# Decoder kernel, fused cross attention and router loop: key rotation over three steps, router work in step 7, narrower scores

## Chip, cores and metric

The kernel runs on one core of one Trainium2 chip, as a single program. The metric is the device time of one execution in microseconds, the median of several runs.

## What is computed

Two decoder blocks over eight sequences (B = 8) of 256 tokens of width 256, with 64 context tokens each. In order: a linear state mixer, cross attention to the context and a ternary-weight gated FFN (block 0); causal self attention, an attention over context and tokens, and a mixture of 32 experts (block 1). The change lies in the last attention and the router of the experts:

```python
q = rms_norm((x @ wq).reshape(B, L, 16, 128), q_norm_w)
k = rms_norm((x @ wk).reshape(B, L, 4, 128), k_norm_w)
k_ctx = rms_norm((h_ctx_kv @ wk_ctx).reshape(B, T, 4, 128), k_norm_w)
q = q * cos + rotate_half(q) * sin
k = k * cos + rotate_half(k) * sin
k_full = concatenate([k_ctx, k]); v_full = concatenate([v_ctx, v])   # 64 + 256 keys
scores = einsum("blhd,bmhd->bhlm", q, k_full) / sqrt(128) + causal mask on the last 256
out = softmax(scores) @ v_full @ wo
x = x + out
...
logits = einsum("bsd,ed->bse", layernorm(x), router_w)     # 32 experts
top1_w, top1_idx = max(softmax(logits)), argmax(logits)
```

## The kernel before

Six phases follow each other: mixer, cross attention, FFN, self attention, **hybrid** (cross attention with rotary keys, and beside it the router of earlier batches), experts. Each engine has its own program, written out by hand; semaphores hold them together. What stands in what order is set by the `hybrid` function of each engine (VectorE L879, POOL L1229, ScalarE L1563, TensorE L2068). Batches 0 to 2 are unrolled, batches 3 to 6 run in a hardware loop of two batches per turn, batch 7 follows it in the same body's last form.

**Units and steps.** A batch has eight steps `i`. Unit `u = 8 * b + i` is one half of the tokens (`j`, steps 0 to 3 and 4 to 7) and one group of four heads (`g`). In step `i` TensorE issues, in this order: scores of tiles 0 and 1 of unit u + 1; the raw query of unit u + 3 (`raw_query`, 4 matmuls of 512 columns); outputs of unit u - 2; scores of tiles 2 and 3 of u + 1; the turned query of u + 2; the turned probabilities of u - 1. In steps 4 and 7 stands `hybrid_out` as well (32 matmuls of 256 columns): in step 4 for the second half of the batch before, in step 7 for the first half of this one. VectorE in step `i`: copies of turned probabilities of u - 2 (L765 to L767), `masked_max` of tiles 0 and 1 of u + 1 (L746), `finish_query` of u + 2 (L728, L732), `normalise` of u (L755, L758), the step's extra work, `masked_max` of tiles 2 and 3, `rotate_query` of u + 3 (L716, L722). Scores lie in two PSUM banks, so the next step's scores wait for the masked maximum of this one; the raw query has one bank, so it waits for the rotation of the one before.

**Tiles of scores.** A tile is 32 tokens by four heads against its keys. `WIDTHS` (L20) gives how many keys each of the four tiles gets: 128, 128, 192, 192 in the first half and 256, 256, 320, 320 in the second. `kmask` adds -1e30 to keys that the token must not see.

**Keys of the next batch.** Three tiles: k = 0 the context (64 keys), k = 1 and k = 2 the tokens. POOL squares and scales them, VectorE sums the squares (`square_key`, L633) in steps 2 to 4 and rotates (`turn_key`, L636), TensorE turns (`turn_keys`, L1865), ScalarE copies the turned tile to its place (`turned_keys`, L1453). Before, VectorE has k = 0 and 1 in step 4 and k = 2 in step 5; TensorE and ScalarE have k = 0 and 1 in step 5 and k = 2 in step 6.

**Router.** For batch b - 1 VectorE has `hybrid_finish` (the residual addition, L772) and `token_stats` (L780, L784) in step 4 and `keep_scales` (L793) in step 6; POOL `token_scales` in step 5; ScalarE `token_norm` (L1544) in step 5. For batch b - 2: TensorE turns the tokens in step 2 and multiplies by the router weights (`route`, 8 matmuls of 32 columns) in step 4; VectorE has `copy_logits` (L799) late in step 5, `choose` (L805 to L816, maximum and index) in step 6 and `keep_weight` (L823) in step 7; ScalarE the exponentials (`weights`) in step 7. In step 5 TensorE waits for the copy of the logits (`f_lg`) ahead of the turned probabilities, since both use bank 7.

## Time and profile before

| what | value |
|---|---|
| median of 3 runs | 1252.36 us (1252.36 to 1252.71) |
| the profiled execution | 1250.75 us, span 1248.9 us |
| TensorE matmul busy | 1060.5 us, 85% of the span |
| VectorE busy | 894.2 us, 72% |
| ScalarE busy | 645.0 us, 52% |
| POOL busy | 324.4 us, 26% |
| one batch of the hybrid loop (885.9 to 970.3) | 84.4 us |

The hybrid phase runs from about 482 to 1156 us. The profile gives each instruction with its start, its length, the idle time of its engine before it and what ended that idle time. In the rows PE is TensorE, DVE is VectorE, ACT is ScalarE; L1663 is the helper that issues every matmul, told apart by its operands (`PS<-wq` raw query, `PS<-wo` hybrid_out, `PS<-EW,arena` scores, `PS<-rwT` router). A matmul's recorded length contains its way through the array, so a rate is read from the distance of starts.

### The profile page before, as it was taken

Reading aid. Unit: us, or ns where it says so; the run is one execution under the profiler, and the core shown is the slowest. Engines: PE = TensorE matmul, PEld = TensorE weight load, DVE = VectorE, ACT = ScalarE, POOL = GpSimd, SP = SyncE. Lnnn points to the kernel's source line nnn. Section 1 sums busy time; section 2 is a strip of 40 time slices with the busy share of each in tenths; the row PEclk is TensorE's granted clock in tenths of the full one; section 3 lists DMA queues with packets and bytes.
Section 4 is the critical chain, followed back from the end, with each engine's and each line's share of the span. In section 5 each row is a group of like instructions: output and inputs, shape, how many; then the busy total and the mean of one; then the engine's idle time right before and its main releaser. Section 6 shows DMA issues by size and latency. Waiting matters only on the chain.

```text
span 1248.9 us, 22083 instructions
## 1 busy us (share of the span) xinstructions
PE 1060.5 (85%) x6399; PEld 729.9 (58%) x6407; DVE 894.2 (72%) x2522; ACT 645.0 (52%) x2011; POOL 324.4 (26%) x496
## 2 busy tenths in 40 slices
PE   3676788689989967989999999899999998998396
PEld 1444345566666644556666666666656666665285
DVE  4576677487788765886867967778678678665375
ACT  0434777455555633655556545555565555552262
POOL 0212321211232121322313213223133132111456
PEclk9955999999999988989999999999999999999598
DMA  9501000112122000400000000000000000000731
GB/s 306 202 0 34 1 1 1 51 53 52 51 58 84 27 1 4 146 1 13 1 6 9 1 14 1 1 14 1 6 9 1 13 1 1 13 1 16 256 91 47
DMA packets 38795, 49.58 MB, mean 40 GB/s; under 512 B 5030, under 2 KB 29484, under 8 KB 38448
## 3 DMA queue, kind: packets, MB, share of 16 engines
q1 hardware_dynamic: 36400, 44.31, 11.9%
q0 software_dynamic: 2304, 4.24, 1.0%
q8 instruction: 35, 0.57, 0.2%
q14 instruction: 56, 0.46, 0.1%
HBM read 32.70 MB, written 14.78 MB: 38 GB/s over the span
## 4 chain that ended last, share of the span: by engine, by line
PE 37%; DVE 11%; issue 6%; POOL 3%; ACT 3%; DMA 0%; DVEq 0%; ACTq 0%; POOLq 0%
PE PS L1663 33%; POOL out_dram L1289 3%; DVE arena L746 2%; DVE arena L758 1%; DVE arena L722 1%; PE PS L2011 1%; PE PS L1988 1%; ACT arena L1505 1%; POOL tokens_dram L1265 1%; ACT arena L1514 1%; DVE arena L732 1%; DVE arena L728 1%; DVE small L780 0%; DVE early L655 0%; DVE early L650 0%
## 5 line engine op out<-in xcount | busy, mean ns | idle before, releaser
L1663 PE MATMUL PS<-EW,arena 128*128 128x128 f32 (+4 forms) x640 | 134.4, 341 | 18.0 <-DVE small L746 11.2
L1663 PE MATMUL PS<-early,arena 128*32 128x256 f32 (+6 forms) x856 | 105.1, 357 | 42.1 <-DVE early L612 23.7
L1663 PE MATMUL PS<-wq,EW 128*128 128x512 f32 x256 | 126.6, 617 | 12.6 <-DVE arena L722 12.3
L1203 POOL TENSOR_SCALAR small<-small 128x4 f32<-128x4 f32 x64 | 18.3, 286 | 427.4 <-ACT mask L1498 250.4
L1663 PEld LDWEIGHTS PS<-EW,arena 128*128 128x128 f32 x640 | 99.6, 193 | 48.9 <-issue 23.5
L746 DVE CUSTOM_DVE_ANT_0 arena<-PS,kmask 128x128 f32<-128x128 f32 (+3 forms) x256 | 92.4, 389 | 42.3 <-PE PS L1663 34.1
L1514 ACT ACTIVATE arena<-arena,small 128x128 f32<-128x128 f32 (+3 forms) x256 | 119.5, 471 | 1.3 <-DVE small L751 1.1
L1505 ACT ACTIVATE arena<-PS 128x512 f32<-128x512 f32 x64 | 38.2, 597 | 153.2 <-PE PS L1988 153.2
L1663 PE MATMUL PS<-wo,early 128*128 128x256 f32 x512 | 113.3, 380 | 2.5 <-DVE sinT L799 1.7
L1663 PEld LDWEIGHTS PS<-wo,early 128*128 128x128 f32 x512 | 97.2, 190 | 16.3 <-DVE sinT L799 2.1
L1663 PEld LDWEIGHTS PS<-early,arena 128*32 128x32 f32 (+3 forms) x864 | 49.8, 115 | 93.3 <-issue 45.5
L1498 ACT ACTIVATE mask<-PS 128x128 f32<-128x128 f32 x256 | 66.7, 274 | 48.5 <-PE PS L1663 47.8
L680 DVE TENSOR_REDUCE small<-PS 128x4 f32<-128x512 f32 x64 | 58.2, 951 | 43.2 <-PE PS L1663 43.2
L1107 POOL TENSOR_SCALAR ve<-mv 128x2 f32<-128x2 f32 x40 | 8.9, 222 | 281.4 <-DVE mv L378 281.0
L1663 PEld LDWEIGHTS PS<-wq,EW 128*128 128x128 f32 x256 | 45.4, 192 | 57.7 <-issue 41.9
L1205 POOL TENSOR_TENSOR small<-small,halves 128x4 f32<-128x4 f32 x64 | 70.3, 1098 | 5.3
L758 DVE TENSOR_SCALAR arena<-arena,small 128x128 f32<-128x128 f32 (+3 forms) x256 | 68.8, 333 | 2.3
L1663 PE MATMUL PS<-arena,EW 128*128 128x512 f32 (+1 forms) x160 | 63.7, 510 | 3.3 <-ACT arena L1521 2.1
L1440 ACT ACTIVATE early<-PS 128x384 f32<-128x384 f32 x64 | 28.5, 488 | 71.3 <-PE PS L1892 71.3
L1479 ACT ACTIVATE arena<-PS,small 128x256 f32<-128x256 f32 x128 | 63.0, 493 | 0.0
L1478 ACT ACTIVATE arena<-PS,small 128x128 f32<-128x128 f32 x128 | 48.8, 381 | 25.7 <-DVE small L680 25.0
L2011 PE MATMUL PS<-ident,arena 128*128 128x128 f32 x384 | 52.8, 274 | 8.3 <-DVE sinT L799 8.3
(310 smaller groups left out, 2467.3 us busy)
## 6 DMA issues: line engine op xcount, KB each, us to landing
EW<-in_masksT_dram SPq DMA_DIRECT2D x32, 256.0 KB, 3.4
tokens_dram<-EW SPq DMA_DIRECT2D x1, 4160.0 KB, 14.9
arena<-tokens_dram SPq DMA_DIRECT2D x16, 260.0 KB, 3.0
results_dram<-EW SPq DMA_DIRECT2D x32, 128.0 KB, 3.2
EW<-results_dram SPq DMA_DIRECT2D x4, 1024.0 KB, 10.5
X<-in_x_dram SPq DMA_DIRECT2D x1, 2048.0 KB, 8.8
wq<-in_wq_dram SPq DMA_DIRECT2D x1, 2048.0 KB, 11.8
wo<-in_wo_dram SPq DMA_DIRECT2D x1, 2048.0 KB, 18.8
```

The lines of the kernel that those rows point to most:

```text
L680: last = dve.tensor_reduce(d_neg[:, i % 2, j, :], PS[:, 0:4, at:at + n], AX.X, ALU.max, negate=True)
L746: dve.tensor_tensor_reduce(probs(i, t), PS[:, 3 + t % 2, 0:n], kmask[:, at:at + n], 1.0, LOWEST, ALU.add, ALU.max, e_max[:, t:t + 1]).then ...
L758: last = dve.tensor_scalar(probs(i, t), probs(i, t), e_inv[:, t:t + 1], None, ALU.mult)
L1205: pool.tensor_tensor(e_rqs[:, i % 2, :], e_q3[:, i % 2, :], halves[:, 0:GH], ALU.pow).then_inc(e_rq, 1)
L1289: pool.indirect_dma_start(out_rows[:, :], bass.IndirectOffsetOnAxis(ap=to, axis=0), sY[:, k, t, :], None, bounds_check=B * S - 1, oob_is_e ...
L1478: act.activation(dP[:, i % 2, r, 0:P], PS[:, r, 0:P], ACT.Exp, bias=d_neg[:, i % 2, 0, r:r + 1])
L1479: act.activation(dP[:, i % 2, r, P:3 * P], PS[:, r, P:3 * P], ACT.Exp, bias=d_neg[:, i % 2, 1, r:r + 1]).then_inc(d_e, 1)
L1498: last = act.activation(eSQ[:, h * XD:(h + 1) * XD], PS[:, 1, h * XD:(h + 1) * XD], ACT.Square, accum_out=e_q2[:, i % 2, h:h + 1])
L1505: act.activation(eQT.rearrange("p (t h q) -> p h t q", t=4, h=GH), PS[:, 2, :].rearrange("p (h t q) -> p h t q", t=4, h=GH), ACT.Copy).the ...
L1514: last = act.activation(tile, tile, ACT.Exp, bias=e_neg[:, i % 2, t:t + 1], accum_out=e_sum[:, i % 2, t:t + 1])
L1663: return pe.matmul(dst, lhs, rhs, start=first, stop=last)
L2011: pe.transpose(PS[:, 5 + k, t * P:(t + 1) * P], eP[:, i % 4, at:at + P], ident[:, :])
```

## The change

- `SEEN` gives the scores' products 96, 128, 160 (first half) and 224, 256, 288 (second half) columns for tiles 0 to 2; tile 3 and everything that reads the scores keep `WIDTHS`.
- `turn_key` (VectorE): k = 0 in step 4, k = 1 in step 5, k = 2 in step 6.
- `turn_keys` (TensorE) and `turned_keys` (ScalarE): k = 0 in step 5, k = 1 in step 6, k = 2 in step 1 of the batch that uses it, in bank 7. TensorE waits for that copy in step 2.
- `token_stats`, `choose` and, behind `hybrid_finish`, `keep_weight` in step 7, `keep_scales` for batch b - 2 in step 1, `copy_logits` at the start of step 5. In the last batch `token_stats` stays in step 4 and `keep_scales` in step 6.
- `token_scales` (POOL) in step 7, `token_norm` (ScalarE) for batch b - 2 at the end of step 0, `weights` ahead of the copied outputs in step 7. In the last batch the first two stay in step 5.

```diff
+SEEN = ((96, 128, 160, 192), (224, 256, 288, 320))
...
+                    if i == 5 and routed:
+                        copy_logits(b - 2, 7)
...
                     if i == 4:
                         if nxt[0] == HYBRID:
                             turn_key(nxt[1], 0)
-                            turn_key(nxt[1], 1)
                         if former:
                             hybrid_finish(b - 1, 1)
+                            if nxt[0] != HYBRID:
+                                token_stats(b - 1)
+                    if 5 <= i <= 6 and nxt[0] == HYBRID:
+                        turn_key(nxt[1], i - 4)
+                    if i == 1 and routed:
+                        keep_scales(b - 2)
+                    if i == 6 and nxt[0] != HYBRID:
+                        keep_scales(b - 1)
+                    if i == 7:
+                        if former and nxt[0] == HYBRID:
                             token_stats(b - 1)
-                    if i == 5 and nxt[0] == HYBRID:
-                        turn_key(nxt[1], 2)
-                    if i == 5 and routed:
-                        copy_logits(b - 2, 7)
-                    if i == 6 and former:
-                        keep_scales(b - 1)
-                    if i == 6 and routed:
-                        choose(b - 2)
-                    if i == 7:
                         if routed:
+                            choose(b - 2)
+                        if nxt[0] == HYBRID:
+                            hybrid_finish(b, 0)
+                            if routed:
+                                keep_weight(b - 2)
+                        else:
                             keep_weight(b - 2)
-                        hybrid_finish(b, 0) if nxt[0] == HYBRID else hybrid_last(b)
+                            hybrid_last(b)
...
-                    if i == 5 and former:
+                    if i == (7 if more else 5) and former:
                         token_scales(b - 1)
...
-                        turned_keys(nxt[1], 1 - par, 2)
+                        turned_keys(nxt[1], 1 - par, 1)
...
-                    if i == 5 and more:
-                        turned_keys(nxt[1], 1 - par, 1)
+                    if i == 1 and former:
+                        turned_keys(b, par, 2, 7)
                     if further[2]:
                         turned_query(u + 2)
-                    if i == 5 and former:
+                    if i == 0 and routed:
+                        token_norm(b - 2)
+                    if i == 5 and not more:
                         token_norm(b - 1)
...
-                        product(PS[:, 3 + t % 2, 0:WIDTHS[j][t]], eQT[:, t * P:(t + 1) * P],
-                                eKT[:, par, g, 0:WIDTHS[j][t]]).then_inc(e_s, 1)
+                        product(PS[:, 3 + t % 2, 0:SEEN[j][t]], eQT[:, t * P:(t + 1) * P],
+                                eKT[:, par, g, 0:SEEN[j][t]]).then_inc(e_s, 1)
...
+                    if i == 1 and former:
+                        turn_keys(b, 2, 7)
...
-                    if i == 5 and more:
-                        pe.wait_ge(e_kc, 3 * b + 4)
-                        turn_keys(nxt[1], 1)
```

How the order of instructions moves, at three places of the loop. Line numbers of the changed kernel are one higher on VectorE and eleven higher on TensorE.

VectorE, end of step 4, before (the rotation of the token tile ends, then the residual addition into X, the statistics, the masked maximum):

```order
L655 TENSOR_TENSOR early<-early 128x512
L658 TENSOR_TENSOR early<-early,small 128x512
L771 ISA
L772 ISA
L772 TENSOR_TENSOR X<-X,PS 128x256
L253 REGISTER_ALU
L207 REGISTER_ALU
L780 ISA
L780 BN_STATS small<-X 128x6 x2
L784 BN_AGGR small<-small 128x2 x2
L207 REGISTER_ALU
L746 ISA arena,small<-PS,kmask 128x320
```

and in the changed kernel (L659 is the last of the context tile's rotation, L773 the addition, L747 the masked maximum):

```order
L659 TENSOR_TENSOR early<-early,small 64x512
L772 ISA
L773 ISA
L773 TENSOR_TENSOR X<-X,PS 128x256
L208 REGISTER_ALU
L747 ISA arena,small<-PS,kmask 128x320
```

The token tile's rotation and the statistics no longer stand around the addition.

VectorE, step 6, before (normalise ends, then keep_scales and choose; the masked maximum follows behind the last row):

```order
L758 TENSOR_SCALAR arena<-arena,small 128x320 x2
L792 REGISTER_ALU
L793 ISA
L793 COPY X<-small 128x2x2
L805 MAX small<-sinT 128x8 x2
L808 TENSOR_SCALAR small<-small 128x2
L810 MAX_INDEX small<-small,sinT 128x8 x2
L813 CAST small<-small 128x2
L816 ISA
L816 TENSOR_SCALAR b_v<-iota,small 128x32
L816 ISA
L816 TENSOR_SCALAR b_v<-iota,small 128x32
```

and in the changed kernel (L647 to L659 are a rotation):

```order
L759 TENSOR_SCALAR arena<-arena,small 128x320 x2
L647 TENSOR_TENSOR early<-early,cosk 128x512
L651 TENSOR_TENSOR early<-early,sink 128x4x64 x2
L655 REGISTER_ALU
L656 TENSOR_TENSOR early<-early 128x512
L659 TENSOR_TENSOR early<-early,small 128x512
L208 REGISTER_ALU
L747 ISA arena,small<-PS,kmask 128x320
```

A rotation stands where keep_scales and choose stood.

TensorE, step 1, before (outputs, the context's keys and values of the next batch, the scores of tile 2):

```order
L1663 MATMUL PS<-arena,w_in 128x512 x2
L1663 MATMUL PS<-arena,w_in 128x256
L1850 REGISTER_ALU
L1663 MATMUL PS<-wvc,eCT 64x512
L1663 MATMUL PS<-wkc,eCT 64x512
L1663 MATMUL PS<-wvc,eCT 64x512
L1663 MATMUL PS<-wkc,eCT 64x512
L253 REGISTER_ALU
L1663 MATMUL PS<-EW,arena 128x192
```

and in the changed kernel (L1876 is `turn_keys`):

```order
L1674 MATMUL PS<-arena,w_in 128x512 x2
L1674 MATMUL PS<-arena,w_in 128x256
L208 ISA
L1876 MATMUL PS<-ident,early 128x128 x4
L1861 REGISTER_ALU
L1674 MATMUL PS<-wvc,eCT 64x512
L1674 MATMUL PS<-wkc,eCT 64x512
L1674 MATMUL PS<-wvc,eCT 64x512
L1674 MATMUL PS<-wkc,eCT 64x512
L254 REGISTER_ALU
L1674 MATMUL PS<-EW,arena 128x160
```

The four transposes of the third tile are new here, and tile 2 has 160 columns in place of 192.

## Rows read from the trace of the kernel before

**Rows 1.** Busy time by stretch, one batch: us, busy us (x) of each engine, PEclk, DMA, GB/s.
```profile
885.90:970.30 84.40, 79.35 (x356) 53.78 (x356) 64.60 (x213) 45.85 (x173) 22.49 (x33) 1.00 0.02 6
```

**Rows 2.** Timeline of TensorE, steps 4 to 7 (start, us, line, op, count [idle before]).
```profile
940.67 7.07 PE L1663 MATMUL PS<-wo,early 128*128 128x256 f32 x32
...
947.58 1.36 PE L1663 MATMUL PS<-EW,arena 128*128 128x320 f32 x6
...
950.41 1.13 PE L1663 MATMUL PS<-EW,arena 128*128 128x256 f32 x4 [0.49 <-DVE small L746]
...
952.38 1.98 PE L1663 MATMUL PS<-wq,EW 128*128 128x512 f32 x4 [0.45 <-DVE arena L722]
...
959.21 1.09 PE L2011 MATMUL PS<-ident,arena 128*128 128x128 f32 x8 [1.49 <-DVE sinT L799]
...
970.34 1.12 PE L1663 MATMUL PS<-wq,EW 128*128 128x512 f32 x2 [1.07 <-DVE arena L722]
```

**Rows 3.** The same timeline, step 0's raw query and step 4's router products.
```profile
901.27 1.88 PE L1663 MATMUL PS<-wq,EW 128*128 128x512 f32 x4
902.99 2.31 PE L1663 MATMUL PS<-arena,w_in 128*128 128x512 f32 x6
...
936.77 0.97 PE L1663 MATMUL PS<-rwT,XT 128*128 128x32 f32 x8
937.58 1.96 PE L1663 MATMUL PS<-wq,EW 128*128 128x512 f32 x4
```

**Rows 4.** Timelines of ScalarE and TensorE, step 1.
```profile
993.89 0.60 ACT L1521 ACTIVATE arena<-PS 128x512 f32<-128x512 f32 x1 [0.30 <-PE PS L2013]
...
996.31 1.88 PE L1663 MATMUL PS<-arena,EW 128*128 128x512 f32 x4
```

**Rows 5.** Timeline of VectorE, batch 1, steps 5 and 6.
```profile
622.09 0.69 DVE L646 TENSOR_TENSOR early<-early,cosk 128x512 f32<-128x512 f32 x1
...
624.83 0.48 DVE L746 CUSTOM_DVE_ANT_0 arena<-PS,kmask 128x320 f32<-128x320 f32 x1
...
631.69 0.20 DVE L793 COPY X<-small 128x4 f32<-128x4 f32 x1
632.23 0.49 DVE L746 CUSTOM_DVE_ANT_0 arena<-PS,kmask 128x320 f32<-128x320 f32 x1 [0.34 <-PE PS L1663]
```

**Rows 6.** Timeline of VectorE in the loop, steps 4 and 6.
```profile
947.91 0.42 DVE L772 TENSOR_TENSOR X<-X,PS 128x256 f32 x1 [2.07 <-PE PS L1663]
...
949.85 0.49 DVE L746 CUSTOM_DVE_ANT_0 arena<-PS,kmask 128x320 f32<-128x320 f32 x1
...
950.27 0.48 DVE L746 CUSTOM_DVE_ANT_0 arena<-PS,kmask 128x320 f32<-128x320 f32 x1
...
966.01 0.20 DVE L793 COPY X<-small 128x4 f32 x1
...
967.81 0.49 DVE L746 CUSTOM_DVE_ANT_0 arena<-PS,kmask 128x320 f32<-128x320 f32 x1
```

**Rows 7.** Batch 0: timelines of TensorE and VectorE, and the stretch at half clock.
```profile
534.50 2.05 PE L1663 MATMUL PS<-EW,arena 128*128 128x256 f32 x4 [3.59 <-DVE small L746]
...
539.68 0.18 DVE L755 RECIPROCAL small<-small 128x4 f32<-128x4 f32 x1 [0.81 <-ACT arena L1514]
...
551.32 0.49 DVE L746 CUSTOM_DVE_ANT_0 arena<-PS,kmask 128x320 f32<-128x320 f32 x1 [0.55 <-PE PS L1663]
...
534.50:541.00 6.50, 6.50 (x13) 3.49 (x14) 5.54 (x19) 2.54 (x10) 0.00 (x0) 0.50 0.01 3
```

**Rows 8.** Timeline of VectorE, batch 2, step 6.
```profile
713.60 0.17 DVE L793 COPY X<-small 128x4 f32<-128x4 f32 x1
...
715.02 0.48 DVE L746 CUSTOM_DVE_ANT_0 arena<-PS,kmask 128x320 f32<-128x320 f32 x1
```

**Rows 9.** Timeline of TensorE, last batch, steps 5 and 7.
```profile
1117.97 1.09 PE L2011 MATMUL PS<-ident,arena 128*128 128x128 f32 x8 [0.81 <-DVE sinT L799]
...
1131.67 1.56 PE L1663 MATMUL PS<-wo,early 128*128 128x256 f32 x6 [1.75 <-DVE sinT L799]
```

More of the change, by code:

```diff
@@ L1590, in hybrid @@
                         query_squares(u + 3, (i + 3) % 8)
+                    if i == 7 and routed:
+                        weights(b - 2)
                     if i >= 2:
@@ L1596, in hybrid @@
                         values(b, par, 1)
-                    if i == 7 and routed:
-                        weights(b - 2)
                     if i == 1 and more:
@@ L2092, in hybrid @@
                     if i == 6 and more:
-                        turn_keys(nxt[1], 2)
+                        turn_keys(nxt[1], 1)
                     if further[3]:
@@ L2108, in hybrid @@
                         keys(nxt[1], 1 - par, 1)
+                    if i == 2 and former:
+                        pe.wait_ge(e_kc, 3 * b + 3)
                     if i == 2 and routed:
@@ L2137, in hybrid @@
                         if i == 5 and more:
+                            pe.wait_ge(e_kc, 3 * b + 4)
+                        if i == 6 and more:
                             pe.wait_ge(e_kc, 3 * b + 5)
-                        if i == 6 and more:
-                            pe.wait_ge(e_kc, 3 * b + 6)
                         if i == 7:
```

## The prediction

> **What bounds the kernel now.** The change touches one phase, the hybrid loop (eight batches of eight steps), so I read the stretches first. A batch in the loop takes 84.4 us, and in it TensorE is busy for 79.35, VectorE for 64.60 and ScalarE for 45.85, at the full granted clock [rows 1]. TensorE paces the loop, with about 5 us per batch in which it stands. The timeline of TensorE shows where [rows 2]: 0.49 before the scores at the start of step 5, 0.45 before that step's raw query, 1.49 before its turned probabilities and 1.07 before the raw query of step 7. Each time the idle time is ended by VectorE: by its masked maximum (L746), its query rotation (L722) and the copy of the logits (L799). So a batch has two parts. From the raw query of step 7 (970.34) to the end of hybrid_out in step 4 (940.67 + 7.07 = 947.74) TensorE sets the time. From there to the next such raw query, 22.6 us, VectorE runs without a pause worth naming and sets it. The two parts have to be costed apart. The end of the second one is what decides the batch.
>
> **TensorE's part: one thing more, one thing less.** The four transposes of the third key tile move from the second part (where TensorE waits anyway) to step 1 (where it doesn't). A matmul instruction of 512 columns takes (902.99 - 901.27) / 4 = 0.43, or 0.84 ns a column [rows 3]. Four transposes of 128 columns therefore add 4 x 0.107 = 0.43 to this part.
>
> The shorter scores take 32 columns from tiles 0 and 2 of every unit; a product is two instructions, so each shortened tile saves 2 x 32 x 0.84 ns = 0.054. That holds for 192, 256 and 320 columns. For tile 0 of the first half (128 to 96) I count nothing: the router's eight products of only 32 columns still take (937.58 - 936.77) / 8 = 0.101 each, almost what 128 columns cost [rows 3], so a floor other than the columns holds there. The Trainium skill, TensorE: Matmul & The Clock Gate, section "Back-to-back issue gap", gives the isolated gap as growing with the columns alone down to 64, by which 96 columns would save that 0.054 too, some 1.7 us in all over 32 units; the same section says that this under-counts where each matmul has a weight load of its own, and the router's row bears that out. In this part fall one shortened tile each of the units scored in steps 7, 0 and 2, two of step 3 and one of step 4; that of step 1 saves nothing, because TensorE then waits for ScalarE's copy of the raw keys. Six times 0.054 is 0.32. TensorE's part becomes 0.43 - 0.32 = 0.11 **longer** per batch.
>
> What else lies in this part is covered. ScalarE's layer norm of the tokens (two instructions, 1.1 us) moves into step 0 ahead of the copy at 993.89, which moves by some 0.8 to 1.1; TensorE's products that read it start at 996.31, so it still lands over 0.7 ahead [rows 4]. If that cover were gone, the excess would be added to every batch. The copy of the turned third tile (0.6) sits in step 1 between the raw keys and the turned query, where ScalarE waits for TensorE. VectorE's keep_scales, and token_stats, choose and keep_weight in step 7, lie beside hybrid_out, for which VectorE waits there anyway; only keep_weight, a reciprocal of two columns, comes behind it, where the next scores are held by TensorE's own turned probabilities.
>
> **VectorE's part in the loop.** Start to start, turn_key of a full tile takes 624.83 - 622.09 = 2.74 [rows 5]. In step 4 it now does one small turn_key beside hybrid_out, then hybrid_finish and at once the masked maximum. Before, that began at 949.85, its second half at 950.27 [rows 6]. Now the second half waits for its scores, which end at 947.58 + 1.36 = 948.94; the hand-over from TensorE to VectorE took 0.17 at hybrid_finish (947.74 to 947.91), so it starts at 949.11. VectorE gains 1.16 us (with token_stats gone, 1.52 was the most it could gain). Through step 5 it keeps them: one full turn_key and one copy of the logits as before, the copy only earlier. TensorE's stands of 0.49 and 0.45 vanish. That of 1.49 loses its releaser, but the next scores need the masked maximum that stands behind turn_key, so it moves there rather than going away. In step 6 keep_scales and choose took 967.81 - 966.01 = 1.80; a turn_key of 2.74 stands in their place, 0.94 more. So the raw query of step 7 comes 1.16 - 0.94 = 0.22 earlier against hybrid_out, and the batch changes by 0.11 - 0.22 = -0.11. Four periods (between the raw queries of step 7 of batches 2 to 6): **-0.4**.
>
> **The other batches.** Batch 0 did both turn_keys in step 4 without a hybrid_out to cover them: TensorE stood 3.59 us, its granted clock fell to 0.50 (1.2 GHz) for the 6.5 us behind, and VectorE then waited 0.81 for ScalarE [rows 7]. With one turn_key per step the same work is spread, that wait and the later one of 0.55 for scores go, and with them what the second half of a masked maximum there waited (0.15) and 0.1 of overlap: **-1.6**, between 0.8 (the first alone) and 1.8. Batch 1 had no choose in step 6, only a short copy and 0.34 of waiting (631.69 to 632.23) [rows 5]: 2.74 - 0.54 = 2.20 more, less 0.15 that the maximum itself no longer waits, less the gain of step 4, here taken as 1.0 (unrolled code has fewer register instructions, so there is less to save; 0.8 to 1.16 in the range): +1.05, with TensorE's 0.11 **+1.2**. Batch 2 had choose, unrolled, in 715.02 - 713.60 = 1.42 [rows 8]: 2.74 - 1.42 - 1.0 + 0.11 = **+0.4**. Batch 7 turns no keys; its 0.81 stand for the logits goes [rows 9], but choose then stands ahead of the copy that releases hybrid_out at 1131.67: 0.3 less, and 0.1 for the third tile: **-0.2**.
>
> The sum is -0.4 - 1.6 + 1.2 + 0.4 - 0.2 = -0.6 us. The profiled execution took 1250.75 us, so it becomes 1250.1; the runs' median of 1252.36 lies 1.6 above the profiled one, so I forecast **1251.7**.
>
> **Rivals.**
> *VectorE hands over later (slower).* The place is the raw query of step 7. The lead won in step 4 has to exceed 0.94 + 0.11 = 1.05; I have 1.16. If something else holds the masked maximum of step 4 or ScalarE's exponentials of step 5 or 6 hold normalise, the lead is eaten and turn_key in step 6 is paid in full. With no lead at all the loop's four periods cost +1.05 each, batch 1 +2.2, batch 2 +1.4, less 1.8 for batches 0 and 7: +6.0, or **1258.4**. For it: the margin is 0.11, and VectorE's chain is unbroken. Against it: no row shows another waiter in step 4. Chance 0.17 (half of the loss would give 1255).
> *TensorE paces all (faster).* If VectorE's longer step 6 were absorbed, the stands of 0.49, 0.45 and 1.49 would all be gained, 2.4 less 0.1 in each of six periods, with batches 0 and 7 some -15 us: **1237**. For it: VectorE is busy only 64.60 of 84.40. Against it: it can't run ahead, since each masked maximum needs the scores of its own step, and its free time lies beside hybrid_out. A part of it is more likely than the whole; chance 0.15.
> *The clock falls.* In the second part TensorE now stands mostly before steps 6 and 7, 1.6 to 1.9 us at a time. A stand of 3.59 was followed by the half clock [rows 7], ones of 1.49 and 1.75 were not [rows 2, 9]. Were 6.5 us at half clock to follow in seven batches, ahead of or in the hybrid_out of step 7, that is 7 x 3.2 = 23 us: **1274**. The Trainium skill, TensorE: Matmul & The Clock Gate, section "HAM oscillation — how this bites in real kernels", tells that an engine that idles between bursts starts each burst at the slow clock; the trace agrees only for the long stand. Chance 0.03.
> *The scores don't get shorter in time*, because the weight loads hold the others too, as they do at 128 columns: +0.32 a batch, +2.3 in all: **1254.0**. Chance 0.07.
>
> **Chances and range.** The forecast's own case has 0.58; its unknowns (the lead in batches 1 and 2, step 6 in the loop, the end) make it 1249 to 1254.5. A measurement of this kernel can tell about 0.2%, 2.5 us. Faster by more: 0.15 and 0.07 of the forecast's case, 0.22. Slower by more: 0.17, 0.03 and 0.07, 0.27. No change: 0.51. The range, with the near halves of the two main rivals, is 1247.5 to 1257.
>
> **What would show it.** In the loop: no stand before the scores of step 5; one of 1.5 to 2 us before the scores of step 6, ended by L747; the raw query of step 7 still waiting about 1 us for the rotation; hybrid_out of steps 7 some 84.3 apart; in batch 0 no half clock near 534; batch 1 longer than 80.9 by about 1. Tile 0's scores of 96 columns as far apart as those of 128. If the spacing of batches moves by more than 0.4 either way, the balance of step 4's gain against step 6's loss was mis-sized; if a wait on ScalarE stands before the turned probabilities or products of step 1, the cover of its moved work was misjudged.

## The result, and the profile after

The changed kernel takes 1261.49 us (median of 4 runs, 1260.17 to 1263.67) beside 1252.53 of the kernel before: ratio 1.007, 95% interval 1.0052 to 1.0087. It is **slower by 9 us**, 4.5 beyond the range's upper end. The profiled execution took 1261.01 (span 1259.1).

I cut both traces at TensorE's raw query in step 7. "Hybrid phase" below is the time from the phase's first raw query to the end of its last hybrid_out: 683.70 before, 691.93 after, so +8.23. (In the 14 traces of this study the phase begins between 470.2 and 476.0 and what follows it takes 91.5 to 93.0, without relation to the kernel; so I compare the phase, and leave what remains of a profile's difference to that spread. Neighbouring batches of the loop differ by up to 0.3 us in the kernel before and by more in the changed one, so a batch is compared with the same batch.)

| stretch | forecast | measured | of it at half clock |
|---|---|---|---|
| batch 0 to its step 7 | -1.6 | -1.90 | none |
| to step 7 of batch 1 | +1.2 | +1.82 | none |
| to step 7 of batch 2 | +0.4 | +0.82 | none |
| four periods of the loop | -0.4 | +4.95 | 1.66 + 1.58 |
| from step 7 of batch 6 on | -0.2 | +2.55 | 1.42 + 1.65 |
| sum | -0.6 | +8.24 | 6.3 |

The largest part is the clock. Busy time by stretch of the changed kernel (us, then busy us and count of PE, PEld, DVE, ACT, POOL, the granted clock, DMA, GB/s), first two loop batches, then the 4 us behind five raw queries of step 7, then the last batch's hybrid_out of step 7:

```profile
892.08:978.32 86.24, 80.53 (x357) 54.36 (x357) 64.67 (x213) 45.43 (x173) 22.29 (x33) 0.98 0.02 6
978.32:1063.07 84.75, 79.03 (x356) 53.72 (x356) 64.43 (x213) 45.53 (x173) 22.53 (x33) 1.00 0.02 5
...
721.30:725.00 3.70, 3.70 (x5) 1.45 (x5) 3.59 (x14) 0.92 (x6) 0.00 (x0) 0.54 0.02 4
892.20:896.00 3.80, 3.80 (x6) 1.63 (x7) 3.69 (x14) 0.96 (x7) 0.00 (x0) 0.58 0.00 0
1063.20:1067.00 3.80, 3.80 (x6) 1.74 (x7) 3.69 (x14) 1.13 (x8) 0.00 (x0) 0.63 0.00 0
807.40:811.20 3.80, 3.80 (x10) 1.86 (x11) 3.69 (x14) 1.85 (x12) 0.45 (x2) 1.00 0.00 0
978.40:982.20 3.80, 3.80 (x10) 1.87 (x11) 3.69 (x14) 1.86 (x12) 0.45 (x2) 1.00 0.00 0
...
1141.20:1150.00 8.80, 8.80 (x33) 7.25 (x33) 1.41 (x11) 0.72 (x4) 0.73 (x3) 0.81 0.00 0
```

In step 7 of batches 2, 4 and 6 the clock falls to near its lower level (1.2 GHz), with 5 or 6 matmuls in the stretch where batches 3 and 5 have 10. The next raw query comes 1.66, 1.58 and 1.42 later for it, and the last batch's hybrid_out takes 8.82 instead of 7.17. Before, no step 7 of the phase was at half clock.

The period with the clock at 1.00, from step 7 of batch 5 to that of batch 6, takes 84.75. The same period before took 84.12 (970.34 to 1054.46; [rows 1] has the one ahead of it), so 0.63 is lost here without the clock. TensorE's timeline there (start, us, line, op, count, idle before and its releaser):

```profile
1020.33 1.07 PE L1674 MATMUL PS<-EW,arena 128*128 128x224 f32 x4 [0.57 <-ACT arena L1514]
...
1040.26 1.30 PE L1674 MATMUL PS<-EW,arena 128*128 128x288 f32 x6
...
1042.85 1.07 PE L1674 MATMUL PS<-EW,arena 128*128 128x224 f32 x4 [0.30 <-ACT arena L1514]
...
1051.44 1.11 PE L1674 MATMUL PS<-EW,arena 128*128 128x224 f32 x4 [1.36 <-DVE small L747]
...
1053.41 1.99 PE L1674 MATMUL PS<-wq,EW 128*128 128x512 f32 x4 [0.43 <-DVE arena L723]
...
1061.10 0.90 PE L1674 MATMUL PS<-EW,arena 128*128 128x96 f32 x4 [1.00 <-DVE small L747]
...
1063.07 3.44 PE L1674 MATMUL PS<-wq,EW 128*128 128x512 f32 x4 [1.07 <-DVE arena L723]
```

The stands moved much as forecast: those of 0.49 and 0.45 in step 5 and that of 1.49 [rows 2] are gone (a smaller one of 0.30, ended by ScalarE, is left there), and 1.36 before the scores of step 6, 0.43 before its raw query and 1.00 before the scores of step 7 came, all on VectorE. The last row's raw query takes 3.44 for 1.98: the half clock begins with it. The shorter scores show too, 1.30 for 1.36 [rows 2] and 1.07 for 1.13; with 96 columns instead of 128 the four products take 0.90 as before. In the kernel before they stood in step 7 as follows, with no stand ahead of them:

```profile
968.36 0.90 PE L1663 MATMUL PS<-EW,arena 128*128 128x128 f32 x4
```

So before, the 1.07 ahead of the raw query of step 7 was the only stand there; the change puts 1.00 ahead of the products just before it.

VectorE's timeline, same batch, steps 4 to 6:

```profile
1040.58 0.42 DVE L773 TENSOR_TENSOR X<-X,PS 128x256 f32 x1 [4.68 <-PE PS L1674]
1041.28 0.49 DVE L747 CUSTOM_DVE_ANT_0 arena<-PS,kmask 128x320 f32<-128x320 f32 x1 [0.28 <-issue]
...
1041.76 0.49 DVE L747 CUSTOM_DVE_ANT_0 arena<-PS,kmask 128x320 f32<-128x320 f32 x1
...
1046.83 0.18 DVE L756 RECIPROCAL small<-small 128x4 f32<-128x4 f32 x1 [0.24 <-ACT arena L1523]
...
1048.17 0.68 DVE L647 TENSOR_TENSOR early<-early,cosk 128x512 f32<-128x512 f32 x1
...
1050.89 0.48 DVE L747 CUSTOM_DVE_ANT_0 arena<-PS,kmask 128x320 f32<-128x320 f32 x1
...
1057.83 0.69 DVE L647 TENSOR_TENSOR early<-early,cosk 128x512 f32<-128x512 f32 x1
...
1060.56 0.48 DVE L747 CUSTOM_DVE_ANT_0 arena<-PS,kmask 128x320 f32<-128x320 f32 x1
```

The lead of step 4 is there: the masked maximum's second half starts 1041.76 - 1040.43 = 1.33 behind the end of hybrid_out (forecast 949.11 - 947.74 = 1.37; before 2.53 [rows 2, 6]), a lead of 1.20. In step 5 normalise then waits 0.24 for ScalarE's exponentials. In step 6 turn_key takes 1060.56 - 1057.83 = 2.73, as costed. And the first row holds what I had not weighed: 4.68 us in which VectorE stands for hybrid_out, 2.07 before [rows 6].

### The profile page after: what moved, and what is told of

The parts are those of the page before. It is cut to its first block, busy times and chain, and to the rows that moved or that the text cites. A ratio compares the mean times of both kernels' runs of the same rounds, so it can differ in the third digit from the quotient of the medians.

```text
span 1259.1 us, 22087 instructions
## 1 busy us (share of the span) xinstructions
PE 1061.9 (84%) x6399; PEld 730.8 (58%) x6407; DVE 894.0 (71%) x2522; ACT 642.8 (51%) x2011; POOL 323.2 (26%) x496
## 4 chain that ended last, share of the span: by engine, by line
PE 36%; DVE 10%; issue 6%; ACT 5%; POOL 3%; DMA 0%; DVEq 0%; ACTq 0%; POOLq 0%
PE PS L1674 33%; POOL out_dram L1298 2%; ACT arena L1523 2%; DVE arena L747 2%; DVE arena L759 2%; PE PS L1999 1%; ACT arena L1514 1%; PE PS L2022 1%; DVE arena L723 1%; POOL tokens_dram L1274 1%; DVE early L656 1%; DVE early L651 1%; DVE early L647 1%; DVE arena L733 1%; DVE arena L729 0%
## 5 line engine op out<-in xcount | busy, mean ns | idle before, releaser
L1674 PE MATMUL PS<-EW,arena 128*128 128x128 f32 (+6 forms) x640 | 129.6, 333 | 31.4 <-DVE small L747 22.6
L1674 PE MATMUL PS<-wq,EW 128*128 128x512 f32 x256 | 129.7, 630 | 14.0 <-DVE arena L723 13.6
L1212 POOL TENSOR_SCALAR small<-small 128x4 f32<-128x4 f32 x64 | 25.1, 392 | 431.8 <-ACT mask L1507 251.0
L747 DVE CUSTOM_DVE_ANT_0 arena<-PS,kmask 128x128 f32<-128x128 f32 (+3 forms) x256 | 92.4, 389 | 42.6 <-PE PS L1674 35.3
L773 DVE TENSOR_TENSOR X<-X,PS 128x256 f32<-128x256 f32 (+1 forms) x16 | 6.7, 422 | 80.6 <-PE PS L1674 80.6
```

Source lines behind the costliest of these rows:

```text
L747: dve.tensor_tensor_reduce(probs(i, t), PS[:, 3 + t % 2, 0:n], kmask[:, at:at + n], 1.0, LOWEST, ALU.add, ALU.max, e_max[:, t:t + 1]).then ...
L1674: return pe.matmul(dst, lhs, rhs, start=first, stop=last)
```

## The experiments

Each kernel was timed beside the kernel before on the same chip; ratios are to it. Theory A is mine at each point. The intervals are 0.1 to 0.2% to either side, so medians of two changed kernels that differ by less than some 2.5 us are not told apart, and there I go by the traces.

| kernel | median us | ratio, 95% interval | hybrid phase | half clock in step 7 of |
|---|---|---|---|---|
| before | 1252.0 | | 683.70 | none |
| changed, again | 1261.08 | 1.0075 [1.0062, 1.0088] | 691.94 | 2, 4, 6, last |
| scores alone | 1251.19 | 0.9992 [0.9981, 1.0002] | 681.42 | none |
| third turn alone | 1255.77 | 1.0028 [1.0017, 1.0040] | 687.39 | none |
| key 1 back in 4 | 1249.19 | 0.9973 [0.9962, 0.9984] | 681.47 | 1, 2, 4, last |
| key 2 in 7 | 1247.07 | 0.9959 [0.9947, 0.9971] | 676.33 | none |
| all beside | 1227.40 | 0.9805 [0.9791, 0.9818] | 659.32 | none |
| filled, 5 and 6 | 1257.66 | 1.0045 [1.0031, 1.0058] | 689.59 | last |
| router alone | 1239.88 | 0.9907 [0.9892, 0.9922] | 670.97 | none |
| choose in 6 | 1276.38 | 1.0199 [1.0173, 1.0224] | 707.87 | 0, 2 to 6 |
| ScalarE's copy later | 1259.82 | 1.0070 [1.0053, 1.0087] | 689.28 | 4, 6, last |
| last batch's choose | 1260.21 | 1.0067 [1.0052, 1.0082] | 689.13 | 1, 5 |
| filled, 6 | 1257.37 | 1.0042 [1.0027, 1.0057] | 692.31 | last |

The last column is for step 7 alone. The half clock of batch 0 in step 5 [rows 7] is there too in every kernel that turns two key tiles in step 4 of batch 0 (before, scores alone, third turn alone, key 1 back in 4, all beside, router alone), and gone in the others. Two more falls in step 6 are named below.

**The two small terms of TensorE.** First the kernel before with the scores' widths alone:

```diff
-product(PS[:, 3 + t % 2, 0:WIDTHS[j][t]], ..., eKT[:, par, g, 0:WIDTHS[j][t]])
+product(PS[:, 3 + t % 2, 0:SEEN[j][t]], ..., eKT[:, par, g, 0:SEEN[j][t]])
```

> The kernel before with the shorter scores alone. Theory A (the prediction's): only the part of a batch that TensorE paces gains, 0.32 us a batch, 2.2 in seven batches: 1250.3 against 1252.5. The traces of after hint at half of it, which would be 1251.4. Theory B (the weight loads hold these products): 1252.5, no change. If the first matmuls of the program come 2.5 us later here too, as in after, that shift is no matter of the hybrid loop.

TensorE's part of a batch (raw query of step 7 to the end of hybrid_out in step 4) is 0.26 to 0.30 shorter in each loop batch, the phase 2.28. So the size of 0.32 nearly holds, and not the half of it at which the expectation hinted. The median's 0.9 alone would not show it: its interval contains 1. The phase begins 0.98 later with nothing changed before it. Then the kernel before with the third key tile's turn moved (on TensorE as below, and ScalarE's `turned_keys` likewise):

```diff
-                    if i == 6 and more:
-                        turn_keys(nxt[1], 2)
+                    if i == 1 and former:
+                        turn_keys(b, 2, 7)
```

> The kernel before with the third key tile turned by TensorE in step 1 of the batch's own pass, nothing moved on VectorE. Theory A: the four transposes move from a stretch in which TensorE waits anyway to one in which it does not, 0.43 us a batch in seven batches: 1255.5 against 1252.5. Theory B (TensorE's part costs more than its own instructions, by waits on ScalarE in steps 1 to 3): 0.6 a batch, 1257. Neither expects the granted clock to fall behind step 7's raw query.

TensorE's part is 0.44 longer in every batch, the phase 3.69, the median 3.7. Both terms of the prediction stand, and their sum is +0.16. The changed kernel's part is +0.13 and +0.45 in turn, its half clock taken off (by the filled kernel below, which has none there). The excess of 0.3 in every second batch is the wait of 0.57 at 1020.33 (0.30 in the neighbouring batches), for ScalarE's copy of the turned query. It is in every kernel that has both the third turn in step 1 and the router's moves, and in neither of the two above nor in the one with the router's moves alone. That copy starts 0.32 after the last record of ScalarE's sequencer ahead of it, in the neighbouring batch 0.05; what it does in between, no record shows.

**VectorE's chain.** The changed kernel with one line moved:

```diff
                             turn_key(nxt[1], 0)
+                            turn_key(nxt[1], 1)
-                    if 5 <= i <= 6 and nxt[0] == HYBRID:
-                        turn_key(nxt[1], i - 4)
+                    if i == 6 and nxt[0] == HYBRID:
+                        turn_key(nxt[1], 2)
```

> The changed kernel with VectorE's turn of the second key tile put back into step 4, where VectorE stands 4.68 us before hybrid_finish; step 5 then turns none, step 6 still turns the third. Theory A (VectorE's chain behind hybrid_out of step 4 sets the raw query of step 7): 2.8 us leave that chain, the raw query of step 7 comes 2.7 earlier in each of six batches, 1261.5 - 16 = 1245; and if the half clock behind it in batches 2, 4 and 6 comes from the stands before steps 6 and 7, it goes too: 1240. Theory B (TensorE's part and not VectorE's is what became longer): less than 1 us a batch is gained, 1256 or more, and the half clock stays.

The second part (hybrid_out in step 4 to the raw query of step 7) goes from 22.65 to 20.33 in every loop batch: 2.32, less than the 2.7 expected, since VectorE now waits for TensorE's scores again (0.15 and 0.16 before masked maxima of steps 4 and 5). It is nearly all that theory A asks of the chain. The median is 1249.19, not 1245: batch 0 takes 3.1 us back, where two key tiles stand in step 4 again. The half clock did not go either: it came in batches 1, 2 and 4. TensorE ahead of step 7's raw query in batch 4:

```profile
885.85 0.90 PE L1675 MATMUL PS<-EW,arena 128*128 128x96 f32 x4 [0.91 <-DVE small L747]
887.83 2.89 PE L1675 MATMUL PS<-wq,EW 128*128 128x512 f32 x4 [1.07 <-DVE arena L723]
```

The stands of 1.36 and 0.43 in step 6 are gone, and these two are left. So one long step of VectorE, the sixth, is enough for the half clock. With the third tile beside hybrid_out of step 7 instead:

```diff
 step 5  turn_key(nxt[1], 1)
-step 6  turn_key(nxt[1], 2)
+step 6  choose(b - 2)
-step 7  token_stats(b - 1); choose(b - 2)
+step 7  token_stats(b - 1); turn_key(nxt[1], 2)
```

> The changed kernel with VectorE's turn of the third key tile in step 7, beside hybrid_out, and choose back in step 6. Theory A: step 6 of VectorE's chain is 1.24 us shorter, 7.4 in six batches: 1254 with the half clock as it is; if the clock falls because of the stands before steps 6 and 7, it stays at 1.00 there and another 4.5 to 6 us go: 1248.5. Theory B (the clock's fall has another cause, in the program's size or in TensorE's own order): the granted clock behind the raw query of step 7 is below 0.7 again in batches 2, 4 and 6, 1254.

The second part is 21.62, 1.03 less for 1.24 taken out, and the clock stays at 1.00 in every batch of the loop: 1247.07. Theory A holds, in one point more narrowly than I had put it: the 1.36, the 0.43 and the 1.07 are all still there, and only the 1.00 before the scores of step 7 is gone. Now the router's moves and the shorter scores without the keys' (TensorE's third turn back in step 6 as well):

```diff
 step 4  turn_key(nxt[1], 0)
+step 4  turn_key(nxt[1], 1)
-step 5  turn_key(nxt[1], 1)
-step 6  turn_key(nxt[1], 2)
+step 5  turn_key(nxt[1], 2)
```

> The changed kernel with the key tiles as before (first and second in step 4, third in step 5, TensorE's third turn in step 6): only the router's work moved and the scores shorter. Theory A: VectorE's chain of the second part is 22.5 - 2.8 = 19.7 us, as with the second tile back in step 4, and TensorE is spared the 0.43 of the third tile: 2.3 less than before in each of six batches, 1252 - 14 = 1238, no half clock. So the router's moves would be the part of the change that helps, and the spreading of the key tiles the part that undoes it. Theory B (the moves of the router bring little alone, since choose and token_stats would only be replaced by waits on TensorE): within 3 us of before, 1249 or more.

It gives 1239.88, 12 us **less** than before. So the change holds a large gain and loses more than that again. And with every extra piece of VectorE beside a hybrid_out:

```diff
+step 4  turn_key(nxt[1], 1); copy_logits(b - 2, 7); choose(b - 2)
-step 5  copy_logits(b - 2, 7); turn_key(nxt[1], 1)
-step 6  turn_key(nxt[1], 2)
-step 7  token_stats(b - 1); choose(b - 2)
+step 7  token_stats(b - 1); turn_key(nxt[1], 2)
```

> The changed kernel with all of VectorE's extra work beside hybrid_out: in step 4 the first and second key tile, the copy of the logits and choose (2.7 + 0.2 + 1.6 us into the 4.68 in which VectorE stands there), in step 7 token_stats and the third key tile (1.2 + 2.8 into some 5.4). Steps 5 and 6 carry none. Theory A (VectorE's chain behind hybrid_out of step 4 is what the loop waits for): that chain falls from 22.5 to 16.9 us, under TensorE's own 18.5, so TensorE paces everything and nearly all its 4 us of stands there go: 3.5 less a batch than before in six batches and about 2 in batch 0, 1252 - 23 = 1229, granted clock 1.00 throughout the loop. Theory B (other waits take the stands' place, ScalarE's turned query or exponentials): half of it, 1240.

1227.40, 24.6 us under the kernel before, the fastest of the study. Busy time of one loop batch of it, and VectorE's timeline in step 4:

```profile
951.75:1032.21 80.46, 78.27 (x356) 53.67 (x356) 64.94 (x213) 45.48 (x173) 22.13 (x33) 1.00 0.02 5
```

```profile
1012.00 0.22 DVE L800 COPY sinT<-PS 128x64 f32<-128x64 f32 x1
1012.37 0.29 DVE L806 MAX8 small<-sinT 128x8 f32<-128x32 f32 x2 [0.15 <-DVE sinT L800]
...
1014.02 0.42 DVE L773 TENSOR_TENSOR X<-X,PS 128x256 f32 x1
1014.55 0.49 DVE L747 CUSTOM_DVE_ANT_0 arena<-PS,kmask 128x320 f32<-128x320 f32 x1
```

TensorE is busy for 78.27 of 80.46, against 79.35 of 84.40 [rows 1]. VectorE does as much as ever (64.94), and fills the wait for hybrid_out to 0.1 us: the addition has no idle time marked any more. The second part is 18.34. Set beside what VectorE does extra in steps 5 and 6 (my sums of turn_key at 2.7, choose at some 1.5 and the copy), the kernels nearly make a line: 5.6 us there give 22.65, 4.4 give 21.62, 2.8 give 20.33 or 20.56, none gives 18.34.

**The clock.** The changed kernel with more work for TensorE in `turn_probs` of steps 5 and 6, of no use (the values are written again behind it):

```diff
                 pe.wait_ge(e_p, v + 1)
+                for t in range(GH if again else 0):
+                    pe.transpose(PS[:, 5, t * P:(t + 1) * P], eP[:, i % 4, STARTS[j][t]:STARTS[j][t] + P], ident[:, :])
+                    pe.transpose(PS[:, 5, t * P:(t + 1) * P], eP[:, i % 4, STARTS[j][t]:STARTS[j][t] + P], ident[:, :])
...
-                        turn_probs(u - 1, (i - 1) % 8)
+                        turn_probs(u - 1, (i - 1) % 8, i in (5, 6))
```

> The changed kernel with eight more transposes by TensorE in each of steps 5 and 6, which write the same values a second time; they fall into its stands of 1.36 and 1.00 us before the scores of the next step. Theory A (the clock falls because TensorE stands there): with more work TensorE keeps 1.00 behind the raw query of step 7 in batches 2, 4 and 6, and the kernel gets 1.6 x 3 = 4.7 us faster: 1256.5. Theory B (the half clock has nothing to do with the stands): half clock as in the changed kernel, 1261.5 or up to 1 us a batch more, 1268.

Its granted clock behind the raw queries of step 7 in batches 2, 4 and 6, and the timeline of TensorE ahead of the last of them:

```profile
719.50:723.30 3.80, 3.80 (x10) 1.86 (x11) 3.69 (x14) 1.95 (x12) 0.46 (x2) 1.00 0.00 0
888.80:892.60 3.80, 3.80 (x10) 1.86 (x11) 3.69 (x14) 1.82 (x12) 0.48 (x2) 1.00 0.02 6
1058.20:1062.00 3.80, 3.80 (x10) 1.84 (x11) 3.69 (x14) 1.78 (x11) 0.53 (x2) 1.00 0.01 2
```

```profile
1046.39 1.11 PE L1674 MATMUL PS<-EW,arena 128*128 128x224 f32 x4 [0.49 <-DVE small L747]
...
1056.06 0.90 PE L1674 MATMUL PS<-EW,arena 128*128 128x96 f32 x4
...
1058.03 1.98 PE L1674 MATMUL PS<-wq,EW 128*128 128x512 f32 x4 [1.07 <-DVE arena L723]
```

The second part is 22.65 to the hundredth, as without the filling, so nothing else moved; the stand of 1.36 shrinks to 0.49, that of 1.00 before the scores of step 7 is no longer marked, and the raw query takes 1.98 again. In batches 2 to 6 this is 4.8 us won by more work. The last batch, where TensorE did not stand at these places, pays 1.4 for it. Another 1.1 is lost in batch 0, but not to the filling: it is there by the phase's fourth raw query (22.12 behind the phase's start for 21.06), ahead of the filled steps, and from there on batch 0 keeps the changed kernel's distances. So the phase is 2.34 shorter in all. With the filling in step 6 alone:

```diff
-turn_probs(u - 1, (i - 1) % 8, i in (5, 6))
+turn_probs(u - 1, (i - 1) % 8, i == 6)
```

> The changed kernel with the eight repeated transposes in step 6 alone, so that only the stand of 1.00 before the scores of step 7 is filled; that of 1.36 before the scores of step 6 and that of 1.07 before the raw query stay. Theory A (the stands add up over the stretch, any one filled is enough): no half clock in batches 2, 4 and 6, 1261.5 - 4.8 + 0.3 = 1257. Theory B (the 1.36 stand counts as well): half clock in at least one of them, 1260.

No half clock in step 7 of batches 2, 4 and 6 either, with the 1.36 and the 1.07 still there. The median is 1257.37, as theory A has it. But the theory's reason, that the stands add up over the whole stretch and any one filled is enough, does not stand: with key 1 back in 4 the 1.36 is gone, and the clock falls all the same. And in this kernel it fell once where nothing was filled, at step 6's raw query of batch 3:

```profile
790.04 1.11 PE L1674 MATMUL PS<-EW,arena 128*128 128x224 f32 x4 [1.36 <-DVE small L747]
...
792.02 3.67 PE L1674 MATMUL PS<-wq,EW 128*128 128x512 f32 x4 [0.43 <-DVE arena L723]
...
792.20:794.20 2.00, 2.00 (x3) 0.88 (x4) 1.96 (x8) 2.00 (x9) 0.00 (x0) 0.50 0.04 8
```

This fall cost nothing: the batch takes 84.50, as with both steps filled, and the stand before its raw query of step 7 is not there. That TensorE would have stood there anyway is my reading of it. The longer phase of this trace (692.31 for 689.59) comes from one stand that no other trace has, behind hybrid_out, and that the profile puts on nothing:

```profile
902.17 0.71 PE L1674 MATMUL PS<-EW,arena 128*128 128x96 f32 x4 [2.56 <-issue]
```

The other direction, a longer stand (choose behind the third turn_key in step 6, out of step 7):

```diff
+                    if i == 6 and routed:
+                        choose(b - 2)
...
-                        if routed:
-                            choose(b - 2)
```

> The changed kernel with choose back in step 6, behind the third key tile's turn: VectorE's step 6 is 1.57 us longer, and TensorE stands about 2.6 before the scores of step 7 instead of 1.0. Theory A (length of the stand decides on the clock): 1.57 in six batches, 9.4, and now the half clock behind every raw query of step 7, 1.6 in three or four more batches: 1276. Theory B (the clock falls by something that comes round every second batch): the half clock stays in batches 2, 4 and 6, 1271.

```profile
988.68 1.22 PE L1674 MATMUL PS<-EW,arena 128*128 128x96 f32 x4 [3.06 <-DVE small L747]
990.65 2.93 PE L1674 MATMUL PS<-wq,EW 128*128 128x512 f32 x3 [0.75 <-DVE arena L723]
...
990.70:996.70 6.00, 6.00 (x10) 2.67 (x11) 4.99 (x18) 2.49 (x16) 0.81 (x2) 0.63 0.00 0
```

The stand before the scores of step 7 is 3.06 in this batch and 2.45 to 3.06 in batches 2 to 6, and the half clock comes in step 7 of all five (batches 0 and 1 choose nothing), at 2.2 to 2.3 us each, and in batch 0: 1276.38, as theory A said. In batch 1 it came in step 6, behind stands of 1.46 and 0.31:

```profile
629.90:632.90 3.00, 3.00 (x4) 1.21 (x4) 2.92 (x10) 2.21 (x9) 0.00 (x0) 0.50 0.01 3
```

What decides between neighbouring batches at the shorter stands was to be seen from the changed kernel once more:

> The changed kernel once more, for a second profile and more times. Theory A (the half clock comes round in one of two neighbouring batches by the program's own rhythm, the start of the hybrid phase does not vary with the kernel): half clock behind the raw query of step 7 in batches 2, 4 and 6 again; the phase starts anywhere between 472.8 and 475.7; 1261. Theory B (chance decides at each stand of this size): other batches at half clock, and times spread by steps of 1.6 us.

```profile
717.40:721.10 3.70, 3.70 (x5) 1.44 (x5) 3.59 (x14) 0.91 (x6) 0.00 (x0) 0.54 0.02 4
888.30:892.10 3.80, 3.80 (x6) 1.63 (x7) 3.69 (x14) 0.96 (x7) 0.00 (x0) 0.58 0.00 0
1059.30:1063.10 3.80, 3.80 (x6) 1.71 (x7) 3.69 (x14) 1.13 (x8) 0.00 (x0) 0.63 0.00 0
```

The same batches, to the same 0.54, 0.58 and 0.63, though the phase began 3.9 us earlier; its length differs by 0.01. Theory A holds for these two traces. Its one fall in two neighbouring batches is no rule: key 1 back in 4 has it in batches 1 and 2, and the next two kernels, with the same stands, in others again. And two traces are few: the six times of this run lie 6.8 us apart, the ten of the kernel before 3.5, so other executions may have fallen elsewhere.

**Two details.** ScalarE's copy behind the exponentials in step 5:

```diff
-                    if i == 5 and more:
-                        turned_keys(nxt[1], 1 - par, 0)
                     exps(u, i)
+                    if i == 5 and more:
+                        turned_keys(nxt[1], 1 - par, 0)
```

> The changed kernel with ScalarE's copy of the turned first key tile in step 5 behind the exponentials, not ahead of them. Theory A (the prediction's lead of 1.16 in step 4 is cut by 0.24 because normalise waits for exponentials that stand behind this copy): that wait goes and the raw query of step 7 comes 0.2 to 0.3 earlier in each of six batches, 1.5 us: 1260. Theory B (TensorE then waits for the copy before its turned query of step 5): no gain or up to 0.5 a batch lost, 1261.5 to 1264.

Normalise no longer waits, and the second part is 22.32 instead of 22.65 in the loop, and 0.39 and 0.27 shorter in batches 1 and 2. That is theory A. The median is 1.3 under that of the changed kernel in the same comparison, which the intervals do not tell apart. Ahead of the last batch the half clock is now in batches 4 and 6 only. And the last batch (choose out of its step 7):

```diff
                     if i == 6 and nxt[0] != HYBRID:
                         keep_scales(b - 1)
+                        choose(b - 2)
```

> The changed kernel with choose of the last batch back in step 6, so that the copy of the logits, which releases the last hybrid_out of step 7, does not stand behind it. Theory A: TensorE stands 1.4 us less there (1.5 instead of 2.9 us), and the 8.8 us of that hybrid_out at a lowered clock fall to 7.2: 3.1 less, 1258.5. Theory B (choose only moves its 1.4 us into step 6, where the scores wait for it): no gain, 1261.5.

TensorE's stand before the last hybrid_out of step 7, in this kernel; in the changed one it was 2.78:

```profile
1137.95 1.35 PE L1675 MATMUL PS<-wo,early 128*128 128x256 f32 x5 [1.34 <-DVE sinT L800]
```

It is 1.44 shorter and hybrid_out takes 7.17, but 0.77 comes back as a new stand before an earlier product, and the half clock now comes in batches 1 and 5: 2.8 less in the phase, 0.9 in the median, within the intervals. Theory A is right in its mechanism; of the 3.1 us that it asked, the median doesn't show that any came. The kernel with the router's moves alone has the stand of 2.78 too and no half clock behind it. So a stand alone does not set it.

## Why the prediction was wrong

**TensorE's part, +0.11.** Its two terms, 0.43 for the transposes and -0.32 for the shorter scores, measured +0.44 and -0.28 alone. The sum was a little low by a term that I put at nothing, since I took ScalarE's moved work as covered: every second batch waits 0.27 more for a copy of ScalarE. Only kernels with both moves have it, so the moved work is the likely cause, but no record shows how. Mean +0.29: missed by 0.2 a batch.

**VectorE's part, -0.22.** The lead of 1.16 measured 1.20, the price of 0.94 in step 6 measured 0.93. In between, 0.24 went to normalise, and some 0.1 more is not accounted for. The failed step is the sum 1.16 - 0.94, which let the whole lead arrive at step 7, and behind it the sentence "Against it: no row shows another waiter in step 4", in the rival that VectorE hands over later: that rival named ScalarE's exponentials of step 5, and it was they. They stand behind a copy of 0.4 in ScalarE's queue, which I had not followed with TensorE's steps moved forward by 1.2. The second part came out at +0.06 or +0.18, in turn. Together 0.41 a batch, or 1.7 us in four periods, instead of -0.4.

**The clock, 0.03.** This is the step that failed most: 6.3 of the 8.2 us. I costed the half clock by one stand of 3.59 in a row [rows 7] and took stands of 1.49 and 1.75 without it [rows 2, 9] as proof that stands of 1.0 to 1.4 are harmless. I took each stand by itself. What counted was a pair: the change puts 1.00 before the scores of step 7, with only those four products between it and the 1.07 before the raw query that was there already. The 14 traces have 98 raw queries of step 7 in batches 0 to 6. Behind the pair (0.91 to 1.11, then 0.98 to 1.07) the clock fell in 14 of 36; with no stand before the scores, and up to 1.07 before the raw query, in none of 57; behind a first stand of 2.45 to 3.06 in all five. The stands further ahead decide little: without the 1.36 it fell (key 1 back in 4), and with it but without the 1.00 it did not in step 7 (key 2 in 7; filled, 6). The Trainium skill, TensorE: Matmul & The Clock Gate, section "A second HAM failure mode: psum-queue depth-cycling", tells of short idles between groups of matmuls, frequent enough that the clock goes back and forth. I had cited the section ahead of it, on long idles. The trace agrees with this one in kind, at 0.54 to 0.63 granted behind the pair of about 1 us each; it gives no length of the idles to compare. My price of 3.2 a batch was too high (1.4 to 1.7 measured), and seven batches too many (three and the last; 7 x 3.2 is 22.4, not 23, but nothing rests on it).

**Batches 0, 1, 2, and the last.** Batch 0 is right (-1.90 for -1.6). Batches 1 and 2 are off by 0.6 and 0.4, from the same lost lead and from TensorE's part. In the last batch, without the clock, -0.5 stands for -0.2.

**The view that I lacked.** I took the two parts of a batch as given, and asked whether step 4's lead covers step 6's loss. The question was where VectorE waits anyway. It stood 2.07 before hybrid_finish with both turn_keys in step 4 [rows 6]: the second was free there. Its move out of step 4 puts a second rotation on the chain, 5.6 us in steps 5 and 6 together, where nothing covers them. The router's moves out of that chain, with the shorter scores, are worth 12 us; the keys' moves on top cost 21, with the half clock and TensorE's third turn in it.

## What to carry to other kernels

Ask of every piece of work that is moved whether it was in the shade of a wait of its own engine, and whether it lands in one; spreading a load evenly over steps is a loss where the steps differ in how long their engine waits. The stretch that an engine sets shrinks with what lies in it, piece by piece, until the next engine's own work is the bound (here 22.6 to 18.3 us). And look at TensorE's stands in pairs: here two of 1 us with 0.9 us of products between them cost a half clock in 14 cases of 36, where a single one of up to 1.07 did not in 57. Work that fills one of the two can be worth its place.

## What the runs showed of the hardware

In step 7 of batches 0 to 6 the granted clock fell to its lower level (1.2 GHz), at 1.4 to 1.7 us lost each time, behind two stands of about 1 us (0.91 to 1.11 and 0.98 to 1.07) with four score products between them: in 14 of 36 cases over all traces, and in none of the 57 without the first of the two. With 2.45 to 3.06 and then 0.60 to 0.75 it fell in all five cases, at 2.2 to 2.3 us each. Twice it fell in step 6, behind 1.36 and 0.43 and behind 1.46 and 0.31. Before the last hybrid_out it fell behind a stand of 2.78 in six traces of seven, and behind 1.34 to 1.75 in none of seven. TensorE did more work in less time when the one stand of 1.00 in step 7 was filled with eight transposes.

With the same stands the same program fell in the same batches in two traces (2, 4 and 6), and edits elsewhere in the program moved it to others (1 and 5; 4 and 6). What chooses the batch was not found. A ScalarE copy that starts 0.3 late in every second batch, with no record of a reason, stays open too.
